# A four-layer image tower on one core: edge rows of the column scatter fetched in four parts through two buffers, and the counting buffer laid over two others

## The reference, cut to what matters

```
src = jnp.concatenate([edge_index[0], loops])
dst = jnp.concatenate([edge_index[1], loops])
...
e_max = jax.ops.segment_max(e, dst, num_segments=M)
ee = jnp.exp(e - e_max[dst])
denom = jax.ops.segment_sum(ee, dst, num_segments=M)
```

## Time and profile before

| | |
|---|---|
| median of 3 runs | 14245.91 us (14245.34 to 14246.84) |
| the profiled execution | 14248.64 us, its span 14246.8 us |
| PE busy | 8506.4 us (60%) |
| PE weight loads busy | 5418.0 us (38%) |
| DVE busy | 6583.8 us (46%) |
| ACT busy | 3350.6 us (24%) |
| POOL busy | 6318.2 us (44%) |
| granted PE clock, mean | 0.716 |
| POOL's column sends | 1150.9 to 3976.7 us, 2112 of them |

### The profile page before, as it was taken

One profiled execution on the slowest core, in us unless ns is written; L12 is line 12 of the kernel. 1 busy time (PEld: TensorE's weight loads), 2 busy tenths in 40 slices (PEclk: granted clock), 3 DMA queues, 4 the chain that ended last, 5 costly groups with the idle time before them and its releaser, 6 DMA issues. The chain is left out here.

```text
span 14246.8 us, 157338 instructions
## 1 busy us (share of the span) xinstructions
PE 8506.4 (60%) x62435; PEld 5418.0 (38%) x62435; DVE 6583.8 (46%) x9074; ACT 3350.6 (24%) x5899; POOL 6318.2 (44%) x6565
## 2 busy tenths in 40 slices
PE   6997798588899967987777774749520000000006
PEld 4775575366667735652222222536310000000004
DVE  5778376200007862139999994452421111111123
ACT  2443343244344432222222221222100000000001
POOL 0005577767710002646666663000036666666640
PEclk8997888788989875559999996555555555555555
DMA  2000000000000000000000001000001111111100
GB/s 102 9 11 18 12 12 11 19 12 20 11 25 9 12 18 10 1 1 2 2 2 2 2 2 1 1 0 0 0 10 19 19 19 17 19 19 19 17 12 7
DMA packets 290069, 178.08 MB, mean 12 GB/s; under 512 B 226797, under 2 KB 274957, under 8 KB 284752
## 3 DMA queue, kind: packets, MB, share of 16 engines
q0 software_dynamic: 209952, 32.71, 3.9%
q1 hardware_dynamic: 79472, 136.16, 3.0%
HBM read 116.87 MB, written 51.56 MB: 12 GB/s over the span
## 5 line engine op out<-in xcount | busy, mean ns | idle before, releaser
L2010 POOL DMA_INDIRECT sorted<-by_row_rows,by_row_idx x2112 | 2031.1, 962 | 2650.9 <-PE bank L1219 1729.1
L2097 POOL DMA_INDIRECT sorted<-r_rows,r_pos x2112 | 2049.9, 971 | 1926.3 <-PE bank L566 1284.5
L2229 POOL DMA_INDIRECT g_g<-table,g_idx x2112 | 2024.7, 959 | 643.6 <-issue 643.6
L1722 DVE TENSOR_TENSOR a_top<-bank,a_k 128x2048 f32<-128x2048 f32 x1024 | 2254.0, 2278 | 6.3 <-ACT a_k L1758 3.8
L2331 PE MATMUL bank<-sc_ident,g_tails 128*20 128x128 f32 x99 | 18.2, 307 | 3136.7 <-PEq L65 3134.9
L1884 PE MATMUL bank<-a_top,sc_pick_row 128*32 128x512 f32 x8192 | 1105.0, 620 | 515.5 <-DVE a_top L1722 492.6
L2331 PEld LDWEIGHTS bank<-sc_ident,g_tails 128*20 128x20 f32 x99 | 7.1, 98 | 3147.6 <-issue 3135.0
L2250 DVE CAST g_nodef<-g_es 128x64 f32<-128x64 int32 x33 | 6.4, 195 | 2492.9 <-DMA g_ep<-sorted 2492.9
L762 DVE TENSOR_TENSOR f_qa<-f_qa,bank 128x512 f32<-128x512 f32 x128 | 82.2, 684 | 2318.6 <-PE bank L556 1982.7
L547 PE MATMUL bank<-f_space,f_proj 128*128 128x512 f32 x2048 | 978.5, 601 | 199.7 <-issue 160.5
L1219 PEld LDWEIGHTS bank<-sw_e_w,e_hid 128*128 128x128 f32 (+1 forms) x4608 | 893.1, 329 | 363.6 <-issue 293.4
(11 more groups left out here) (467 smaller groups left out, 13013.8 us busy)
## 6 DMA issues: line engine op xcount, KB each, us to landing
f_stage<-folded SPq DMA_DIRECT2D x16, 2304.0 KB
sorted<-r_rows,r_pos POOLq DMA_INDIRECT x2112, 2.1
sorted<-by_row_rows,by_row_idx POOLq DMA_INDIRECT x2112, 2.1
g_g<-table,g_idx POOLq DMA_INDIRECT x2112, 2.6
states<-g_st SPq DMA_DIRECT2D x33, 768.0 KB
fp_raw<-t_modes SPq DMA_DIRECT2D x4, 2304.0 KB, 15.0
folded<-fp_turned SPq DMA_DIRECT2D x4, 2304.0 KB, 7.8
f_bb<-t_features SPq DMA_DIRECT2D x4, 2048.0 KB, 11.4
```

Of the source, the lines that this page charges most:

```text
L1722: v.tensor_tensor(top[:, n % RD].rearrange("p q (h s) -> p q h s", s=S), q, kk, ALU.max).then_inc(top_done, 1)
L2010: p.indirect_dma_start(out=self.dst, out_offset=bass.IndirectOffsetOnAxis(ap=self.idx[:, k:k + 1], axis=0), in_=self.rows[:, k, :], in_off ...
L2097: p.indirect_dma_start(out=self.dst, out_offset=bass.IndirectOffsetOnAxis(ap=self.pos[:, k // PART_STEPS, at:at + 1], axis=0), in_=self.ro ...
L2229: p.indirect_dma_start(out=g[:, k_in, j, :], out_offset=None, in_=d["table"], in_offset=bass.IndirectOffsetOnAxis(ap=idx[:, k_in, j:j + 1] ...
```

## The change

Rows are fetched in four parts of 528 columns, each through one of two buffers that hold 528 columns: 4 loads in place of 48, of 4,224 bytes for each partition in place of 352. Parts 0 and 1 are issued at the start. Part 2 stands in SP's order at chunk `send_at(19) // 8` = 25, part 3 at `send_at(31) // 8` = 33; they wait on all eight `sent` semaphores, part 2 for the sends of the first 12 steps, part 3 for those of the first 24. POOL's step k waits for the part k // 12 and for the same y steps as before. The store of a ranked part (`place_part`) moves: part 0 from chunk 13 to 12, part 1 from 21 to 20, parts 2 and 3 stay at 29 and 37. `ranks.nodes` goes away: the column-sorted edges are loaded into the first of the two row buffers. `run` and `posf` become the halves of one tile, `work`, and `seen` is that tile read as bf16. The transfers of POOL, DVE's operations, and everything on PE and ACT stay the same in number, size and order.

The diff:

```diff
@@ -372,10 +372,12 @@
                         sp.wait_ge(used, yi(u, 0, 0))
                     sp.dma_start(proj[:].rearrange("p c o y -> p (c o y)"), f.projections[u % LAYERS]).then_inc(proj_in, 16)
 
-                def rows(k):
-                    if k >= 2:
-                        sp.wait_ge(sent[(k - 2) % HD_SENDS], 16 * STEP_COLS * ((k - 2) // HD_SENDS + 1))
-                    sp.dma_start(ranks.rows[:, k % 2], ranks.edges[:, k * STEP_COLS:(k + 1) * STEP_COLS, :]).then_inc(rows_in[k % 2], 16)
+                def rows(part):
+                    if part >= 2:
+                        done = PART_STEPS * (part - 1)
+                        for j in range(HD_SENDS):
+                            sp.wait_ge(sent[j], 16 * STEP_COLS * len(range(j, done, HD_SENDS)))
+                    sp.dma_start(ranks.rows[:, part % 2], ranks.edges[:, part * QC:(part + 1) * QC, :]).then_inc(rows_in[part % 2], 16)
 
                 def place_part(part):
                     sp.wait_ge(placed, part + 1)
@@ -387,7 +389,7 @@
                         sp.wait_ge(place_out, 16 * PARTS)
                     else:
                         sp.wait_ge(nodes_used, part)
-                    sp.dma_start(ranks.nodes[:], ranks.by_column[:, part * QC:(part + 1) * QC, :]).then_inc(nodes_in, 16)
+                    sp.dma_start(ranks.rows[:, 0], ranks.by_column[:, part * QC:(part + 1) * QC, :]).then_inc(nodes_in, 16)
 
                 def row_part(part):
                     sp.wait_ge(row_placed, part + 1)
@@ -411,11 +413,11 @@
                         n = u * CHUNKS + ch
                         if ch == 2 and last_of(u) and u + 1 < UNITS:
                             group_in(u // LAYERS + 1)
-                        for k in range(SEND_STEPS - 2):
-                            if (send_at(k) + 4) // 8 == n:
-                                rows(k + 2)
-                                if k % PART_STEPS == 1:
-                                    place_part(k // PART_STEPS)
+                        for part in range(PARTS):
+                            if n == send_at(PART_STEPS * part + 1) // 8:
+                                place_part(part)
+                            if part >= 2 and n == send_at(PART_STEPS * part - 5) // 8:
+                                rows(part)
                         if n == ROW_CHUNK:
                             for part in range(PARTS):
                                 nodes(part)
@@ -437,7 +439,7 @@
             def _(p):
                 for k in range(SEND_STEPS):
                     p.wait_ge(placed, k // PART_STEPS + 1)
-                    p.wait_ge(rows_in[k % 2], 16 * (k // 2 + 1))
+                    p.wait_ge(rows_in[k // PART_STEPS % 2], 16 * (k // PART_STEPS // 2 + 1))
                     p.wait_ge(y_done, send_at(k) + 1)
                     ranks.send(p, k, 0, STEP_COLS // 2, sent[k % HD_SENDS])
                     p.wait_ge(y_done, send_at(k) + 4)
@@ -747,7 +749,7 @@
                             continue
                         ranks.rank(v, c, part, i)
                         if i == bins - 1:
-                            c.link(v.tensor_copy(ranks.pos[:, part], ranks.posf[:]))
+                            c.link(v.tensor_copy(ranks.pos[:, part], ranks.posf))
                             v.sem_inc(done, 1)
 
                 for u in range(UNITS):
@@ -2058,19 +2060,18 @@
         self.by_column = d["sorted1"].rearrange("(p c) w -> p c w", p=P)
         self.end = d["starts"][NODES:NODES + 1].rearrange("(a b) -> a b", b=1)
         self.key = sb("key", [P, COLS], BF16)
-        self.seen = sb("seen", [P, COLS], BF16)
         self.hit = sb("hit", [P, QC], BF16)
-        self.run = sb("run", [P, QC])
-        self.posf = sb("posf", [P, QC])
+        work = sb("work", [P, 2, QC])
+        self.run, self.posf = work[:, 0, :], work[:, 1, :]
+        self.seen = work[:].rearrange("p a c -> p (a c)").bitcast(BF16)
         self.pos = sb("pos", [P, PARTS, QC], I32)
-        self.nodes = sb("nodes", [P, QC, 2], I32)
+        self.rows = sb("rows", [P, 2, QC, 2], I32)
         self.hist = sb("hist", [P, P])
         self.base = sb("base", [P, P])
         self.ends = sb("ends", [P, 1], I32)
-        self.rows = sb("rows", [P, 2, STEP_COLS, 2], I32)
 
     def count(self, v, c, i):
-        c.link(v.tensor_scalar(self.seen[:], self.key[:], self.t.iota[:, i:i + 1], None, ALU.is_equal, ALU.add, accum_out=self.hist[:, i:i + 1]))
+        c.link(v.tensor_scalar(self.seen, self.key[:], self.t.iota[:, i:i + 1], None, ALU.is_equal, ALU.add, accum_out=self.hist[:, i:i + 1]))
 
     def offsets(self, v, c, bins, shift):
         below, total, base = self.t.bank[4][:, 0:bins], self.t.bank[5][:, 0:bins], self.base[:, 0:bins]
@@ -2083,19 +2084,19 @@
     def rank(self, v, c, part, i):
         key = self.key[:, part * QC:(part + 1) * QC]
         c.link(v.tensor_scalar(self.hit[:], key, self.t.iota[:, i:i + 1], None, ALU.is_equal))
-        c.link(v.tensor_tensor_scan(self.run[:], self.hit[:], self.hit[:], self.base[:, i:i + 1], ALU.add, ALU.bypass))
+        c.link(v.tensor_tensor_scan(self.run, self.hit[:], self.hit[:], self.base[:, i:i + 1], ALU.add, ALU.bypass))
         v.tensor_copy(self.base[:, i:i + 1], self.run[:, QC - 1:QC])
-        c.link(v.copy_predicated(self.posf[:], self.hit[:].bitcast(mybir.dt.uint16), self.run[:]))
+        c.link(v.copy_predicated(self.posf, self.hit[:].bitcast(mybir.dt.uint16), self.run))
 
     def row_key(self, v, c, part):
-        c.link(v.tensor_scalar(self.run[:].bitcast(I32), self.nodes[:, :, 1], 7, None, ALU.logical_shift_right))
-        c.link(v.tensor_copy(self.key[:, part * QC:(part + 1) * QC], self.run[:].bitcast(I32)))
+        c.link(v.tensor_scalar(self.run.bitcast(I32), self.rows[:, 0, :, 1], 7, None, ALU.logical_shift_right))
+        c.link(v.tensor_copy(self.key[:, part * QC:(part + 1) * QC], self.run.bitcast(I32)))
 
     def send(self, p, k, lo, hi, sent):
         for j in range(lo, hi):
             at = k % PART_STEPS * STEP_COLS + j
             p.indirect_dma_start(out=self.dst, out_offset=bass.IndirectOffsetOnAxis(ap=self.pos[:, k // PART_STEPS, at:at + 1], axis=0),
-                                 in_=self.rows[:, k % 2, j, :], in_offset=None).then_inc(sent, 16)
+                                 in_=self.rows[:, k // PART_STEPS % 2, at, :], in_offset=None).then_inc(sent, 16)
 
 
 def clamp_edges(t, d, rank):
@@ -2119,7 +2120,7 @@
             def _(v):
                 c = Chain(v, own)
                 c.link(v.memset(minus[:], -1))
-                c.link(v.memset(rank.posf[:], 0.0))
+                c.link(v.memset(rank.posf, 0.0))
                 v.wait_ge(loaded, 16)
                 c.link(v.tensor_copy(node[:], edges[:, :, 1]))
                 c.link(v.tensor_scalar(mask[:], node[:], 0.0, float(1 << 20), ALU.is_lt, ALU.mult))
```

## The result

| | before | changed |
|---|---|---|
| median | 14246.38 us, 4 runs | 13856.28 us, 4 runs (13845.88 to 13858.17) |
| ratio | | 0.9724 (0.9707 to 0.9741) |
| span of the profiled execution | 14246.8 us | 13854.9 us |
| first load behind the spectral stage | 5256.3 us | 4860.0 us |

The changed kernel is 390 us faster; 13,851 us were forecast, from 13,825 to 13,895. The stage ends 396.3 us earlier, and the rest of the program takes 4.4 us longer than before, which is less than the changed kernel's own runs differ by (12.3 us).

A forecast was written before the change was run, and what follows sets the result against it. PE and its chain bound the spectral stage, held up by SP's fixed order behind late POOL. Gains 211.7 + 160.5 + 30.6 = 402.8 us, less 8 at chunk 50, give 395 us: 13851 us, range 13,825 to 13,895.

The forecast's parts named there:

- The three waits: PE's waits in the spectral stage: 211.7 us for result stores, 160.5 us for projections, 62.2 us in group prologues.
- "issue" at L547: PE's five waits with no named releaser, 160.5 us, read as the projection missing behind SP's loads of rows.
- The sum: Spectral stage: stores 211.7, projections 160.5 and prologues 30.6 us gained, 402.8 us, all before chunk 50.
- chunk 50: DVE held up 6 to 11 us there for `nodes` because POOL ends late; 8 us taken, reaching PE in full.
- Restart: Some 2 us more gained per long PE wait removed, 0 to 13 us; 0 taken, 13 kept for the range.
- Costs put at nothing: Larger loads at the start, parts 2 and 3, stores of ranked parts, shared count buffer: cost 0 each.
- The layout of the count buffer: Shared count buffer on DVE: same instructions on the same engine and chain, in one order; cost 0.
- Rival (1): Denser PE and DVE work slows POOL's sends; DVE waits about 40 us at chunk 50: 13,883 us; chance 0.14.
- rival (5): Change does nothing; projection and store are late for another reason than SP's order: 14,246 us; chance 0.01.

The follow-up runs named there:

- waits_last: Changed kernel with the old single-step waits put back in units 3 and 7 alone: 16880.8 us, 0.9989 of the kernel before; repeated, 16890.2 us, 1.0000.
- the slowed pair: Kernel before and changed kernel, each with POOL waiting after every 11 sends until they have landed: 14479.9 and 14138.6 us.
- changed_again: The changed kernel unaltered, on a chip where the kernel before takes 16889.5 us: 16894.6 us, ratio 0.9999.

## Why the prediction was right

**What bounds the kernel.** Right. The three waits that I read from the earlier trace rows went, and unit 6 became shorter by 50.5 us where its wait had been 50.4 us. That "issue" at L547 was the missing projection is shown twice: it left with the waits, and it doubled when POOL was made slower.

**The sum.** 402.8 us less 8 us for chunk 50 were forecast. At unit 12's first projection matmul, the last mark ahead of chunk 50's cost, the changed kernel is 403.0 us ahead. At unit 12's blend, the first mark behind both, the changed kernel is 4358.9 - 3964.6 = 394.4 us ahead. DVE waited 9.1 us for 8 forecast; POOL's last send ended at 3842.4 us for 3840 to 3844.

**Restart.** I took 0 of a possible 13 us. As a sum that came true, but not for my reason, and chance may have a part in it. The slow start behind a wait is there. In unit 6 of the kernel before, PE's first four projection matmuls behind the 50.4 us took 3.75 us and the 16 that follow 3.08 us; in the changed kernel, without the wait, 1.88 and 1.92 us. Before, and then changed, with the stretches of 6.8 us from the first of them below:

```profile
2199.13 3.08 PE L556 MATMUL bank<-f_from_y,f_space 128*128 128x96 f32 x16
...
2025.38 1.88 PE L549 MATMUL bank<-f_space,f_proj 128*128 128x512 f32 x4
2027.10 1.92 PE L558 MATMUL bank<-f_from_y,f_space 128*128 128x96 f32 x16
```

```profile
2195.50:2202.30 6.80, 6.72 (x21) 4.65 (x22) 0.00 (x0) 0.06 (x1) 5.13 (x6) 0.56 0.74 305
...
2025.40:2032.20 6.80, 6.80 (x29) 4.04 (x28) 6.56 (x11) 3.03 (x5) 5.28 (x6) 1.00 0.02 1
```

The granted clock behind the wait was 0.56 of full speed, mostly the lower of its two levels (1.2 and 2.4 GHz), and 1.00, the upper one, without the wait. From the first projection matmul to its blend unit 6 took 210.9 us before and 207.9 us changed, 3.0 us less. But the opening of the same unit, from the last blend to that matmul, took 82.7 us in the changed kernel and 79.8 us before (without the wait), 2.9 us more. The five units that had waited for a projection show the same two amounts: 12.9 us less in sum behind the wait, 12.8 us more ahead of it. Why the openings became longer no run tells. They also differ by 1.9 to 2.5 us between the two traces in units 1 to 3, where the kernels had no such wait, one longer and two shorter, so the balance may be chance. For the same reason the 2.2 us that I read as the price of a restart (290.7 against 288.5 us) were no measure of it: units 1 and 2 of the changed kernel take 291.3 and 286.0 us. The Trainium skill's rule of the half-rate restart (TensorE: Matmul & The Clock Gate, "Part 1: The HAM clock gate") agrees with the rows behind the wait; the 13 us that I worked out beside it did not reach the sum.

**Costs put at nothing.** The parts were issued at 1958.6 and 2531.5 us (forecast: from 1943 us, and 2450 to 2530 us) and SP waited 0.4 us for sends in all. Nothing behind them in the queue was held up. The layout of the count buffer was not run alone; the marks before 1080 us, 1067.4 us before and 1066.8 us now at the third blend, leave it no price there.

**Rival (1).** The denser work did not slow the sends: a send took (3841.4 - 1148.4) / 2111 = 1.276 us on average, between the 1.289 and 1.261 us of the earlier trace rows, and unit 5 still held 225 sends in 290.6 us.

**What the prediction did not see.** It took POOL's pace against PE's as given. That is the condition of the whole gain, and on four of the five chips of the experiments it does not hold: in the trace of every kernel that ran there POOL waits for y steps 40 times or more. The changed kernel itself ran on one of the four and is worth nothing there (0.9999). My rival (5), that the change does nothing, had 1 in 100 and for another reason. The 390 us are shown for the kind of chip on which the kernel before takes some 14,250 us.

**What stays open.** Whether the costs of blocked stores and blocked projections add up by place (14,098 us for `waits_last`) or are one lateness (14,164 us) was not decided, since both tries fell where neither costs. So did the direct separation of waits from loads. For that the slowed pair stands in, with the 0.32 us of a load's issue: the old order is 341 us slower than the new one, with the waits in the rows that SP feeds.

## What to carry to other kernels

In a queue that issues in order, a wait for a slow engine delays every later transfer, and the engine that pays may have nothing to do with either: look for waits with no named releaser and compare their ends with the queue's timeline. A buffer deep enough that its wait is long satisfied when the queue comes to it turns many small delays into one, at the place where the data is needed. Such a gain depends on which engine is ahead of which; work that pays on one chip may pay nothing where the order of the two is turned.

## What the runs showed of the hardware that I had not expected

The same program took 14,254 us on one chip and 16,889 to 17,046 us on four others, with PE at a mean granted clock of 0.72 and 0.67. Most of the difference lies where the two scatters send: the second one (L2012) takes 3,104 us in the changed kernel and 4,245 us in `changed_again`. The third set of 2,112 indirect transfers, the gathers at L2230, takes 3,096 and 3,099 us, so not every such stretch is slower. In `changed_again` the projections of SP's queue mark the ends of units. The three pairs enclose unit 2 (no sends yet), unit 5 (sends) and unit 13 (sends over):

```profile
769.63 0.32 SPq L373 DMA_DIRECT2D f_proj<-projections  x1
1060.05 0.32 SPq L373 DMA_DIRECT2D f_proj<-projections  x1
...
2101.43 0.32 SPq L373 DMA_DIRECT2D f_proj<-projections  x1
2616.74 0.32 SPq L373 DMA_DIRECT2D f_proj<-projections  x1
...
5848.68 0.32 SPq L373 DMA_DIRECT2D f_proj<-projections  x1
6141.39 0.32 SPq L373 DMA_DIRECT2D f_proj<-projections  x1
```

A unit takes 290.4, 515.3 and 292.7 us. On the fast chip it takes 290.6 us with sends. While sends run there, engines wait for work of others that has long ended; the profile calls these waits "remote". ACT's waits in the same run, up to 5500 us:

```profile
ACT f_space L674 <- remote: 1244.4, 68, 41.5
...
ACT f_space L668 <- remote: 521.3, 36, 42.8
```

Such "remote" rows do not stand in the fast chip's answers. One of these waits in the timeline, with POOL's last send before it:

```profile
2295.61 0.96 POOL L2098 DMA_INDIRECT sorted<-r_rows,r_pos  x1 [0.30 <-issue]
...
2303.17 0.49 ACT L674 ACTIVATE f_space<-bank 128x384 f32<-128x384 f32 x1 [37.33 <-remote]
2303.24 1.28 DVE L764 TENSOR_TENSOR f_qa<-f_qa,bank 128x512 f32<-128x512 f32 x2 [89.56 <-remote]
...
2304.19 0.53 PE L532 MATMUL bank<-f_to_x,f_bb 96*96 96x128 f32 x1 [30.79 <-ACT f_space L668]
```

PE had ended its work at 2273.4 us, so what ACT and DVE waited for was done 30 us before; both go on in the same tenth of a microsecond, 6.6 us after POOL's last send of that step had been issued. In unit 5 DVE and ACT are busy 210.2 and 124.0 us, as in the changed kernel on the fast chip (210.8 and 125.9); PE is busy 321.5 us against 278.9 us, at a granted clock of 0.74 against 0.92. POOL needs 958 ns to issue a send on both. So the sends seem to delay the signals between engines, and not to lengthen the work of DVE, ACT and POOL; that is my reading of these rows and not shown by a run of its own. What differs between the chips no run here tells.
